# Threshold search of an expert router: rounds on 23-bit whole numbers, each count split between VectorE and ScalarE

## What is computed

```python
B, S, H = x.shape                      # 16, 548, 128
bs = B * S                             # 8768 tokens
E = NUM_EXPERTS                        # 32
k = min(int(bs * C_CAP) // E, bs)      # 274 tokens for each expert
xf = x.reshape(bs, H)
h = xf @ W_router + b_router
Sm = jax.nn.softmax(h, axis=-1)
G_ek, idx_ek = jax.lax.top_k(Sm.T, k)  # each expert takes the 274 tokens of highest probability
tokens = xf[idx_ek]
...
y = jnp.zeros((bs, H), dtype=x.dtype).at[idx_ek.reshape(-1)].add(weighted.reshape(-1, H))
```

## Time and profile before

| | us |
|---|---|
| median of 3 runs | 2126.67 |
| lowest and highest | 2124.03, 2128.3 |
| the profiled execution, its own time | 2130.16 |
| span of that execution in the trace | 2128.3 |
| from the start of `choose_tokens` (about 589.5) to the first expert's transfers (815.9) | 226.4 |
| of that, the loop of 21 rounds, from 607.70 to 695.75 | 88.05 |

### The profile page before, as it was taken

One profiled execution on the slowest core, in us unless ns is written; L12 is line 12 of the kernel. 1 busy time (PEld: TensorE's weight loads), 2 busy tenths in 40 slices (PEclk: granted clock), 3 DMA queues, 4 the chain that ended last, 5 costly groups with the idle time before them and its releaser, 6 DMA issues. The chain is left out here.

```text
span 2128.3 us, 31340 instructions
## 1 busy us (share of the span) xinstructions
PE 1544.4 (73%) x9132; PEld 1081.9 (51%) x9132; DVE 1318.0 (62%) x2105; ACT 744.3 (35%) x1369; POOL 719.1 (34%) x758
## 2 busy tenths in 40 slices
PE   5779999998701004776627558888888658999998
PEld 3457777775301003555514423333333457788787
DVE  3845555555577892111115777777777657989988
ACT  2235555555300001333203346677666321111111
POOL 1345555552000014788753012222231113323332
PEclk8679999999855556989858889999999859999999
DMA  4050000000210002444450000000000000000000
GB/s 137 0 232 1 0 0 0 0 0 0 74 32 0 1 1 52 85 78 81 64 150 28 4 2 2 0 0 0 0 0 0 1 32 8 11 11 15 11 15 14
DMA packets 69696, 60.85 MB, mean 29 GB/s; under 512 B 15789, under 2 KB 63675, under 8 KB 68363
## 3 DMA queue, kind: packets, MB, share of 16 engines
q1 hardware_dynamic: 52174, 47.52, 6.9%
q0 software_dynamic: 15744, 11.85, 4.1%
q10 hardware_dynamic: 1728, 0.85, 0.1%
HBM read 35.06 MB, written 25.18 MB: 28 GB/s over the span
## 5 line engine op out<-in xcount | busy, mean ns | idle before, releaser
L1610 DVE TENSOR_SCALAR at_clip<-at_slot 128x548 bf16<-128x548 f32 (+1 forms) x320 | 226.4, 722 | 79.7 <-PE at_slot L1453 72.8
L1541 ACT ACTIVATE at_clip<-at_slot,at_four 128x548 bf16<-128x548 f32 (+1 forms) x320 | 226.6, 713 | 126.9 <-PE at_slot L1453 125.0
L1453 PE MATMUL at_slot<-at_qm,at_ks 128*128 128x274 bf16 (+1 forms) x1280 | 216.9, 285 | 55.2 <-ACT at_clip L1541 45.7
L1591 POOL TENSOR_SCALAR at_qm<-at_qs,at_headmask 128x548 bf16<-128x548 bf16 x128 | 97.1, 777 | 360.6 <-DVE at_qs L1619 360.6
L1453 PEld LDWEIGHTS at_slot<-at_qm,at_ks 128*128 128x128 bf16 (+1 forms) x1280 | 90.7, 97 | 150.4 <-ACT at_clip L1541 90.7
L1188 DVE TENSOR_SCALAR ex_y<-ex_ps_y,ex_rows 128x128 f32<-128x128 f32 (+1 forms) x96 | 29.2, 346 | 216.2 <-PE ex_ps_y L1135 106.0
L467 PE MATMUL ga_kv<-ga_kern,ga_v 128*128 128x274 f32 x512 | 132.1, 400 | 14.3 <-ACT ga_kern L552 13.7
L2042 DVE TENSOR_REDUCE mx_routed<-mx_weighted 128x128 f32<-128x1024 f32 x69 | 137.6, 1995 | 2.4
L1092 POOL DMA_INDIRECT moe_sums<-ex_y,slot_sums x80 | 124.8, 1560 | 34.6 <-issue 21.3
L612 POOL TENSOR_TENSOR ga_rot<-ga_by_cos,ga_by_sin 128x274 f32<-128x274 f32 (+1 forms) x96 | 70.1, 730 | 168.0 <-DVE ga_by_sin L656 168.0
L1134 PE MATMUL ex_ps_y<-ex_down,ex_hid 128*128 128x128 f32 (+3 forms) x576 | 99.7, 325 | 34.3 <-ACT ex_hid L1175 22.2
(11 more groups left out here) (346 smaller groups left out, 3800.7 us busy)
## 6 DMA issues: line engine op xcount, KB each, us to landing
moe_sums<-ga_zeros SPq DMA_DIRECT2D x8, 1152.0 KB, 18.9
ar_rows<-moe_sums SPq DMA_DIRECT2D x32, 256.0 KB
ex_down<-in_down SPq DMA_DIRECT2D x32, 192.0 KB
out_h<-H SPq DMA_DIRECT2D x22, 192.0 KB, 1.9
H<-in_text SPq DMA_DIRECT2D x1, 4096.0 KB, 20.9
token_rows<-tr_rows SPq DMA_DIRECT2D x16, 256.0 KB
patches<-in_patches SPq DMA_DIRECT2D x1, 1728.0 KB, 7.8
ga_sin<-in_sin SPq DMA_DIRECT2D x1, 1644.0 KB, 10.2
```

The costliest lines, as they stand in the source:

```text
L1453: last = nc.tensor.matmul(slot[SLOT[T % 2][u]][0:rows_of(t), s, 0:HALF], ks[p][:, t * P:t * P + rows_of(t)], qm[p][:, h, j * HALF:(j + 1) ...
L1541: nc.scalar.activation(clip[T % 2][u][0:r], slot[SLOT[T % 2][u]][0:r, :, 0:HALF], ACT.Relu, bias=four[0:r], scale=-1.0).then_inc(by_act, 1)
L1591: last = nc.gpsimd.tensor_scalar(qm[p][:, h, :], qs[:], headmask[:, h:h + 1], 1.0, ALU.mult, ALU.mult)
L1610: nc.vector.tensor_scalar(clip[T % 2][u][0:r], slot[SLOT[T % 2][u]][0:r, :, 0:HALF], 4.0, None, ALU.min).then_inc(by_dve, 1)
```

## The change

The search is rewritten in four ways.

1. **Whole numbers.** The bit patterns are shifted right by 7 (`LOW`), which leaves 23-bit whole numbers, and turned into float32 (`keys`). `EARLY` is 23 now, so the first part of the search covers all of them. The trial value is a whole number less one half, so that no key ever equals it.
2. **Split count.** In each round DVE counts in 1344 columns (`ON_DVE`); at the same time ACT computes the sign of trial minus key over the other 864 columns and sums the signs into `signs`. PE adds both into one PSUM total by two matmuls: `half_expert` (`same_expert` times -0.5) with the signs, then `same_expert` with the count. The comparison is with 274 - 4 * 432, since each column on ACT gives plus or minus one half in place of 1 or 0.
3. **Next trial.** DVE computes trial + step/2 while PE works (`raised`), and from the total `lost` = step or 0; the next trial is `raised` - `lost`. Before, four small operations stood between two counts (`won`, `found`, `bit`, `cand`); now two do (`lost`, `trial`).
4. **Written out.** The 23 rounds are unrolled; there is no loop around them. After them the trial is turned back into a bit pattern (a conversion and a shift left). The full count, `open_` and the rounds left stand as before; if an expert is still open there are now 7 of those in place of 9, and otherwise 1 as before.

Four semaphores are added. `load_inputs` and `gated_attention` now clear theirs when they end, and give them back to be used again.

The core of the diff:

```diff
@@ load_inputs, gated_attention
-        sem = lambda n: st.enter_context(nc.semaphore(f"in_{n}"))
+        sem = lambda n: nc.alloc_semaphore(f"in_{n}")
...
+    nc.clear_and_free_semaphores([img_in, text_in, const_in, embedded, evacuated, bias_in, cut, laid])
...
+    nc.clear_and_free_semaphores(used)
@@ choose_tokens
-        EARLY = 21
-        N1 = EARLY + 2
+        EARLY = 23
+        N1 = 2
+        LOW = BITS - EARLY
+        ON_DVE = 1344
+        ON_ACT = SEGP - ON_DVE
...
-            nc.vector.memset(bit[:], 1 << (BITS - 1))
-            nc.vector.memset(found[:], 0)
+            nc.vector.memset(bit[:], 1 << (LOW - 1))
+            nc.vector.tensor_scalar(half_expert[:], k["same_expert"][:], -0.5, None, ALU.mult)
+            nc.vector.memset(trial[:], float(1 << (EARLY - 1)) - 0.5)
...
-            s0 = chain[0]
-            with dve.Fori(0, EARLY) as i:
-                narrow(i, s0 + 4 * i, step, counted, summed)
-            chain[0] += 4 * EARLY
-
+            link(nc.vector.tensor_single_scalar(V[:].bitcast(I32), PR[:].bitcast(I32), LOW, ALU.logical_shift_right))
+            link(nc.vector.tensor_copy(keys[:], V[:].bitcast(I32)))
+            nc.vector.memset(keys[:, SEG:SEGP], -1.0).then_inc(trial_set, 1)
+            dve.wait_ge(trial_set, 1)
+            for i in range(EARLY):
+                step_of = float(1 << (EARLY - 1 - i))
+                nc.vector.tensor_scalar(mark[:, 0:ON_DVE], keys[:, 0:ON_DVE], trial[:], None, ALU.is_ge, ALU.add, accum_out=cnt[:]).then_inc(by_dve, 1)
+                nc.vector.tensor_scalar_add(raised[:], trial[:], step_of / 2)
+                dve.wait_ge(trial_summed, i + 1)
+                link(nc.vector.tensor_scalar(lost[:], tot[:, 0:1], float(TOPK - NGRP * ON_ACT // 2), step_of, ALU.is_lt, ALU.mult))
+                nc.vector.tensor_tensor(trial[:], raised[:], lost[:], ALU.subtract).then_inc(trial_set, 1)
+                dve.wait_ge(trial_set, i + 2)
+            link(nc.vector.tensor_copy(found[:], trial[:]))
+            link(nc.vector.tensor_single_scalar(found[:], found[:], LOW, ALU.logical_shift_left))
...
@@ on ScalarE, behind the exponential
+            for i in range(EARLY):
+                act.wait_ge(trial_set, i + 1)
+                if i > 0:
+                    act.wait_ge(trial_summed, i)
+                nc.scalar.activation(junk[:], keys[:, ON_DVE:SEGP], ACT.Sign, bias=trial[:], scale=-1.0, accum_out=signs[:]).then_inc(by_act, 1)
@@ on TensorE
-            with pe.Fori(0, EARLY) as i:
-                total(i, counted, summed)
-            total(EARLY, counted, summed)
-            pe.wait_ge(counted, EARLY + 2)
+            for i in range(EARLY):
+                pe.wait_ge(by_act, i + 1)
+                nc.tensor.matmul(tot[:, 0:1], half_expert[:], signs[:], start=True, stop=False)
+                pe.wait_ge(by_dve, i + 1)
+                nc.tensor.matmul(tot[:, 0:1], k["same_expert"][:], cnt[:], start=False, stop=True).then_inc(trial_summed, 1)
+            total(0, counted, summed)
+            pe.wait_ge(counted, 2)
```

More of the change, by code:

```diff
@@ L329, in _ @@
             nc.vector.tensor_copy(k["pick_row_r"][:], k["pick_row"][:])
+    nc.clear_and_free_semaphores([img_in, text_in, const_in, embedded, evacuated, bias_in, cut, laid])
 def gated_attention(nc, k, x, H, HN, moe_d):
+    used = []
     with ExitStack() as st:
@@ L341, in gated_attention @@
         ps = lambda n, s: st.enter_context(nc.psum_tensor(f"ga_{n}", s, F32))
-        sem = lambda n: st.enter_context(nc.semaphore(f"ga_{n}"))
+        sem = lambda n: used.append(nc.alloc_semaphore(f"ga_{n}")) or used[-1]
         cos = sb("cos", [P, 3, S])
@@ L848, in choose_tokens @@
         BITS = 30
-        EARLY = 21
-        N1 = EARLY + 2
+        EARLY = 23
[3 more added lines that the diff above has]
+        ON_ACT = SEGP - ON_DVE
+        keys = sb("keys", [P, SEGP])
+        signs = sb("signs", [P, 1])
+        trial = sb("trial", [P, 1])
+        raised = sb("raised", [P, 1])
+        lost = sb("lost", [P, 1])
+        junk = sb("junk", [P, ON_ACT], BF16)
+        half_expert = sb("half_expert", [P, P])
+        trial_set, by_dve, by_act, trial_summed = (sem(n) for n in ("trial_set", "by_dve", "by_act", "trial_summed"))
         block = st.enter_context(nc.Block())
@@ L887, in narrow @@
                 dve.wait_ge(step, at + 4)
-            s0 = chain[0]
-            with dve.Fori(0, EARLY) as i:
-                narrow(i, s0 + 4 * i, step, counted, summed)
-            chain[0] += 4 * EARLY
+            link(nc.vector.tensor_single_scalar(V[:].bitcast(I32), PR[:].bitcast(I32), LOW, ALU.logical_shift_right))
[12 more added lines that the diff above has]
+            link(nc.vector.tensor_single_scalar(found[:], found[:], LOW, ALU.logical_shift_left))
             nc.vector.tensor_scalar(mark[:], PR[:], found[:].bitcast(F32), None, ALU.is_ge, ALU.add, accum_out=cnt[:]).then_inc(counted, 1)
-            dve.wait_ge(summed, EARLY + 1)
+            dve.wait_ge(summed, 1)
             nc.vector.tensor_scalar(open_[:], tot[:, 0:1], float(TOPK), None, ALU.is_gt).then_inc(counted, 1)
-            dve.wait_ge(summed, EARLY + 2)
+            dve.wait_ge(summed, 2)
             link(nc.vector.reduce_max(n_left_f[:], blk_ps[:], AX.X))
```

## The result

Measured side by side, the changed kernel takes 2103.05 us (median of 6 runs, 2099.27 to 2105.59) and the kernel before 2127.17 (6 runs, 2122.59 to 2128.87). The ratio is 0.989, with a 95% interval of 0.9876 to 0.9905: 24.1 us less, between 20.2 and 26.4. The forecast was 22.1 less, 2104.6 us, in a range of 2101 to 2111. The profiled execution of the changed kernel took 2103.82 us with a span of 2102.0.

A forecast was written before the change was run, and what follows sets the result against it. The prediction took the search to be one serial path across the engines. The search's -22.8 us, +0.2 for `half_expert` and +0.5 for the clears gave -22.1, from a median of 2126.67 to 2104.6 us, range 2101 to 2111.

The forecast's parts named there:

- One serial path: In the search, nothing runs beside the chain of count, total, decision and next trial; every microsecond counts in full.
- the gain given back in the experts' stage: Rival after the search: TensorE's clock rises later once the experts run, putting the time at 2115 us; chance 0.03.
- DVE's side of the round: In each search round, 1344 columns at 1.046 ns on DVE give a round of 2.70 us in place of 4.20.
- ACT's side: In each round, ACT's pass of 1.01 us and its matmul stay hidden behind DVE's count, 0.12 us to spare.
- The upper end of 1.48: In each round, latest start of the sign matmul after the trial, in us, with ACT's accumulator read at 0.38.
- Around the rounds: Setup, 23 rounds and way back to a bit pattern: shift taken at 1.31 us, full count 22.8 us earlier.
- `half_expert` and the clears: At the stage's start and two barriers: about 0.2 us for the 128x128 pass, 0.25 for each semaphore clear.
- The sum of the steps that could be sized, 22.8: From the memset through the rounds, the full count was to start 22.8 us earlier.
- the caution of 0.7: Costs booked against the gain outside the rounds: 0.2 us for making `half_expert`, 0.5 for the two semaphore clears.
- ACT's side setting the round: Rival in each round: sign matmul later than 1.30 us after the trial; round 2.88, time 2108.7; chance 0.12.
- the rounds left: Rival behind the search: an expert still open, 7 old rounds in place of 1, 25.2 us more; chance 0.02.
- the double rate: Rival in DVE's count: whole numbers run at 0.55 ns a column, round 2.58, time 2101.8 us; chance 0.03.

The follow-up runs named there:

- dve_1088: The changed kernel with 1088 columns counted on VectorE and 1120 on ScalarE, in place of 1344 and 864; 2109.28 us, ratio 0.9893 to the kernel before.
- dve_1272: The changed kernel with 1272 columns counted on VectorE and 936 on ScalarE, in place of 1344 and 864; 2106.82 us, ratio 0.9888 to the kernel before.
- fp32r_1168: The changed kernel with both matmuls of a round in float32r, 1168 columns on VectorE and 1040 on ScalarE; 2099.42 us, ratio 0.9865.
- unrolled_only: The kernel before with its 21 rounds written out and nothing else changed; 2122.41 us, ratio 0.9964.
- clears_only: The kernel before with only the two semaphore clears added, at the ends of load_inputs and gated_attention; 2130.64 us, ratio 1.0002.
- rounds_21: fp32r_1168 with GpSimd's iota put behind the first transpose and 21 rounds in place of 23; 2092.89 us, ratio 0.9818 to the kernel before.

## Why the prediction was right

By its own steps:

- **One serial path.** Right. 23.2 us went from the search, and the stretches up to the first gather are no longer than before, at the same clock of 0.50. For the gain given back in the experts' stage: it takes 257.6 to 260.5 us in the kernels with a shorter search, the profiled 253.23 apart, and 258.86 before. Nothing above about 2 us came back there; behind it the rest swings too much to tell.
- **DVE's side of the round.** 1.68 + 0.62 + 0.20 + 0.20 = 2.70; the trace has 1.68, 0.63, 0.19 and 0.19, 2.69. The column at 1.046 ns gave a count of 1.61, and 1612 ns were measured. Over 23 rounds the difference makes 0.3 us (61.8 in place of 62.1).
- **ACT's side.** The pass was put at 1.01 and took 1015 ns. The accumulator read takes 186 ns in place of the 84 of DVE, but starts 0.09 before the pass is recorded as ended, so that the sign matmul stands at 1.16, where 1.18 was expected. The upper end of 1.48 was far off. The margin to DVE's side was real but thinner than told, and one reading in it was wrong: the 0.38 of the earlier trace rows runs from the first matmul to the second one's weight load (717.57), not to the second matmul (717.64), which is 0.45. With that the sum gives 1.63 against DVE's 1.68, 0.05 to spare in place of 0.12, and ACT's side would set the round from 1.23 on, not from 1.30. Measured it is 1.16, and 0.07 are left; dve_1088 and dve_1272 bear out the 0.45. That the slip changed nothing was in part luck: had the accumulator come at its upper end of 1.48, the round would have grown by 0.25, not by 0.18.
- **Around the rounds.** The shift at 1310 ns was the lower end, as chosen. Search and setup together 65.5 expected, 65.11 measured.
- **`half_expert` and the clears.** Booked with 0.7 us, they cost 0.1. The transpose began 0.16 behind the first memset in place of 0.07, although the pass is recorded with 1.91 us; that GpSimd's iota would stretch the pass was not foreseen, and in fp32r_1168 the same thing did cost 1.5 us. The clears added nothing at either barrier.
- **What was missing.** 0.95 us behind the search: the entry to the MAX8 loop takes 1.07 in place of 1.47 (from `dummy` to the first MAX8), and the draws are 0.55 shorter. The table shows the 0.40 in every kernel whose search is written out, unrolled_only among them, and not in clears_only. So it goes with the missing loop; how was not tested. The draws behave the same way: 88.10 and 88.18 in the two kernels with the loop, 87.39 to 87.75 in all others. The entry before and after:

```profile
723.32 2.46 DVE L938 MAX8 ct_top<-ct_order 128x8 f32<-128x2208 f32 x1 [1.25 <-issue]
...
699.06 2.46 DVE L962 MAX8 ct_top<-ct_order 128x8 f32<-128x2208 f32 x1 [0.85 <-DVE ct_dummy L956]
```

The sum of the steps that could be sized, 22.8, was 0.4 short; the caution of 0.7 and the unforeseen 0.95 make up the rest to 24.1. So the path and the price of a round were right, and 1.6 of the 2.0 us by which the gain was missed lie outside the search. In the time only 1.5 us of them show (2103.05 against 2104.6), because the kernel before came out 0.5 higher than in the runs that the forecast started from. Of the rivals, ACT's side setting the round was made to happen by 256 columns more, the rounds left cost what was said when forced, and the count didn't take the double rate: 1612 ns for 1344 columns are one column in 1.046 ns and the same fixed part as the earlier trace rows, whole numbers or not. With that the Trainium skill's tier table ("VectorE: DVE Perf Modes", section "The perf-mode tier table (the rule you actually need)") holds here for the shift, 1310 ns for 2208 columns (of int32, where the table has fp32), and not for the form that also sums.

The experiments add what the prediction left open, the shares: 0.90 of the 1.51 us saved in a round come from the split, 0.36 from the loop, 0.25 from the shorter choice of the next trial. The whole-number form costs 2.8 us of setup and, as EARLY was raised with it, two rounds of 2.69. The two rounds weren't needed on this data: rounds_21 takes them back.

## What to carry to other kernels

In a serial loop over several engines, cut one round at the starts of its links, price each link from rows of its own kind, and compute when each leg reaches the meeting point; here that gave the round to 0.01 us. When two legs meet at TensorE, balance them with the spacing of queued matmuls in mind, and look at the number of passes of the matmul itself: for one column of small whole numbers dropping the float32 format's second pass was worth 4.9 us, more than any further balancing (under 1). Judge such a change by its own stretch of the trace, since the rest of a long program swings by more than a few us.

## What the runs showed of the hardware

- A VectorE pass of one source within SBUF (128x128 float32, 0.23 us alone) is recorded with 1.91 us beside a GpSimd iota of 1.97, and ends 0.08 behind it. A 32x32 block transpose of VectorE ran its full 2.47 us during the same iota, with no delay. The Trainium skill has this rule in "SBUF — State Buffer", section "SBUF: two separate sides": a VectorE operation in a mode with two ports and a GpSimd operation lock each other out of a shared port pair for a whole instruction. The trace agrees: of four such operations in fp32r_1168 each ended 0.08 to 0.16 behind the iota, and with the iota moved they took 0.16 to 0.23. Ports and modes themselves no trace here shows.
- ACT's accumulator read is 186 ns, of which about 0.09 overlap the pass; DVE's is 84.
- A total of one column by matmul in float32 occupies 0.58 us at the 1.2 GHz clock, in the reduced format 0.37 with two columns. A queued second total loads 0.38 and starts 0.45 behind the first in float32, at most 0.19 and 0.24 in the reduced format.
- Idle time ahead of the first instruction of a hardware loop's body was put down to the last semaphore waited for. From the halved bit to the next candidate it is 0.53 us in the loop (615.59 to 616.12) and 0.18 with the rounds written out, and a round is 0.36 shorter.
